# Two mixture-of-experts tile loops: routing tables on partitions, edge scores inside the routing inversion, two shared expert products moved from the head of the second loop to its end

## The reference, cut to what matters

```python
x = x + tanh(g_xattn[0]) * L0_attention(layernorm(x), ctx)          # 1024 rows of 256
x = x + tanh(g_ffn[0])  * L0_moe(layernorm(x))     # 8 experts, inner width 688, top 2 of each row
x = x + tanh(g_xattn[1]) * (0.6*sigmoid(si[:,None] + sj[None,:] + b) + 0.4*layernorm(x))
x = x + tanh(g_ffn[1])  * L1_moe(layernorm(x))     # 15 routed experts, top 2, and one shared expert
# an expert:  silu(x @ w_gate.T) * (x @ w_up.T) @ w_down.T
# shared expert of L1 (inner width 176): applied to every row, added without a routing weight
```

## Time and profile before

| | us |
|---|---|
| median of 3 runs | 369.81 (369.34 to 369.99) |
| the profiled execution, whole | 369.4 |
| its span | 367.4 |
| outside the span (369.4 - 367.4) | 2.0 |
| PE busy in the span | 322.0 (88%) |
| DVE / ACT / POOL busy | 205.4 / 153.1 / 109.4 |
| chain that ended last | PE 76%, DVE 11%, ACT 4%, issue 4%, DMA 2% |

### The profile page before, as it was taken

How to read it: one execution, slowest core, us unless ns; L and a number is a source line. 1 busy time by engine, 2 the same in 40 slices (tenths; PEclk the granted TensorE clock), 3 DMA queues, 4 the chain that set the end, 5 groups by cost and what they waited for, 6 DMA issues and landing times.

```text
span 367.4 us, 6937 instructions
## 1 busy us (share of the span) xinstructions
PE 322.0 (88%) x2144; PEld 185.0 (50%) x2144; DVE 205.4 (56%) x640; ACT 153.1 (42%) x339; POOL 109.4 (30%) x106
## 2 busy tenths in 40 slices
PE   8974599899999999999999999158878999989992
PEld 6643493555555555555555555047334444444440
DVE  1678874655554445555555542495936645455237
ACT  1565402133444343343344444267433545445541
POOL 0021131221333332222212221133234666563310
PEclk9995556999999999999999999655869999999995
DMA  7999919996927372554211112411222222331146
GB/s 236 346 309 319 299 40 287 282 271 199 239 38 245 81 214 41 164 122 133 31 37 14 16 14 29 93 38 59 72 58 55 75 88 87 83 77 58 45 145 228
DMA packets 21146, 48.40 MB, mean 132 GB/s; under 512 B 2600, under 2 KB 11688, under 8 KB 20088
## 3 DMA queue, kind: packets, MB, share of 16 engines
q1 hardware_dynamic: 14680, 35.78, 31.0%
q0 software_dynamic: 6048, 11.28, 14.4%
q10 hardware_dynamic: 384, 0.90, 0.8%
HBM read 37.98 MB, written 9.96 MB: 131 GB/s over the span
## 4 chain that ended last, share of the span: by engine, by line
PE 76%; DVE 11%; ACT 4%; issue 4%; DMA 2%; POOL 1%; ACTq 1%; another core or an unknown queue 1%; DVEq 0%; POOLq 0%
PE bank L1432 27%; PE bank L1406 23%; PE bank L1482 8%; PE bank L1396 6%; PE bank L1245 3%; PE bank L1253 3%; PE bank L1305 2%; DVE st L749 1%; DVE z L939 1%; DMA sums<-y_sb,route_dst 1%; DVE z L827 1%; PE bank L1374 1%; DMA rows<-sums 1%; PE bank L1325 1%; POOL fs L403 1%
## 5 line engine op out<-in xcount | busy, mean ns | idle before, releaser
L1432 PE MATMUL bank<-wgu,xT 128*64 x320 | 99.5, 465 | 1.5 <-issue 0.9
L1432 PE MATMUL bank<-rows,xT 128*64 128x344 f32 x320 | 99.5, 465 | 0.0
L1406 PE MATMUL bank<-wdn,hT 120*64 (+2 forms) x396 | 89.9, 392 | 8.5 <-ACT hT L583 6.8
L1406 PEld LDWEIGHTS bank<-wdn,hT 120*64 120x64 f32 (+1 forms) x396 | 48.9, 140 | 48.4 <-issue 23.0
L1432 PEld LDWEIGHTS bank<-wgu,xT 128*64 128x64 f32 x320 | 43.1, 140 | 47.5 <-issue 8.2
L423 POOL DMA_INDIRECT sums<-y_sb,route_dst x20 | 31.6, 1581 | 115.5 <-ACT y_sb L621 97.5
L415 POOL DMA_INDIRECT x_in<-rows,route_tok x43 | 42.7, 993 | 46.3 <-DVE route_tok L945 17.6
L1019 DVE SCALAR_TENSOR_TENSOR hh<-th,bank 128x344 f32<-128x344 f32 x40 | 20.5, 513 | 58.2 <-ACT th L571 58.2
L1406 PE MATMUL bank<-rows,hT 120*64 120x256 f32 x228 | 52.4, 379 | 0.0
L1432 PEld LDWEIGHTS bank<-rows,xT 128*64 128x64 f32 x320 | 43.1, 140 | 0.0
L571 ACT ACTIVATE th<-bank 128x344 f32<-128x344 f32 x40 | 18.3, 458 | 59.3 <-PE bank L1432 59.3
(11 more groups left out here) (172 smaller groups left out, 451.6 us busy)
## 6 DMA issues: line engine op xcount, KB each, us to landing
wgu<-gu SPq DMA_DIRECT2D x8, 1376.0 KB, 22.4
wdn<-wd SPq DMA_DIRECT2D x8, 720.0 KB, 27.0
wgu<-gu SPq DMA_DIRECT2D x3, 1408.0 KB, 7.1
wdn<-wd SPq DMA_DIRECT2D x5, 576.0 KB, 8.3
rows<-rows SPq DMA_DIRECT2D x8, 256.0 KB, 3.7
wgu<-results SPq DMA_DIRECT2D x4, 512.0 KB, 5.0
wgu<-gu SPq DMA_DIRECT2D x1, 1056.0 KB, 6.8
rows<-xt SPq DMA_DIRECT2D x4, 256.0 KB, 7.4
```

What stands on the lines that cost most here:

```text
L1406: last = mm(psum[7][part, 0:H], hT[0:m.wide, j * P:(j + 1) * P][:, part], wd(j), start=(j == 0), stop=(j == m.chunks - 1))
L1432: last = mm(psum[2 * c + g][part, 0:CH0], xT[:, r, k * P:(k + 1) * P][:, part], w, start=(k == 0), stop=(k == KH - 1))
```

## The change

- `owners` puts the slots' numbers on partitions: one compare of 40x7 (46x14) elements and one sum that writes the integer table; PE, ACT and DVE load an expert's number from the slot's partition.
- Ahead of loop 1, `targets` and `weights` move behind the first staging of weights; the edge scores run between the steps of the inversion in place of the fillers, and `keep_warm(2)` is gone.
- Ahead of loop 2, `owners` comes before the second `hidden_early`; `scale_scores` is split, `shared_terms` stays early and the rest comes later; the second turn of x (`turn_x(1)`) stands ahead of the first slot product; six semaphores for the weights become one.
- `AHEAD = 2`: only row tiles 0 and 1 of the shared expert have their down product at the head. The products of 2 and 3 are kept (`kept_h`) and stand at the end with those of 4 to 7: six downs, in which the turn and copy of the next stand ahead of the down (two banks, two halves `hT1`).
- The results come back by eight DMAs of one row tile each, and `combine` works by row tile, its second instruction waiting for its first.

```diff
@@ owners
-                then(nc.vector.tensor_tensor(
-                    m.scmp[0:1], cf[0:1, C_SLOT:C_SLOT + 2 * m.S].unsqueeze(2).to_broadcast([1, 2 * m.S, E - 1]),
-                    m.incl[0:1, 0:E - 1].unsqueeze(1).to_broadcast([1, 2 * m.S, E - 1]), ALU.is_ge))
-                then(nc.vector.tensor_reduce(out=m.ownf[0:1, :], in_=m.scmp[0:1], axis=X, op=ALU.add))
-                nc.vector.tensor_copy(m.owner[0:1, :], m.ownf[0:1, :]).then_inc(m.experts_ready, 1)
+                halves = 2 * m.S
+                then(nc.vector.tensor_scalar(m.passed[0:halves], m.incl[0:halves, 0:E - 1],
+                                             cf[0:halves, C_ROW:C_ROW + 1], None, ALU.is_le))
+                    nc.vector.tensor_reduce(out=m.owner[0:halves], in_=m.passed[0:halves], axis=X,
+                                            op=ALU.add).then_inc(m.experts_ready, 1)
@@ inverse and what followed it (PE)
-                    if m.n == 0 and i % 2 == 1 and i < 2 * NT - 4:
-                        mm(psum[1][:, 0:D], ones, filler[:, 0:D], start=True, stop=True)
+                    if m.n == 0 and i % 2 == 0:
+                        si = mm(psum[5][:, tile:tile + 1], ctx_all[:, tile * P:(tile + 1) * P], wi, start=True, stop=True)
-            for i in range(NT):
-                last = mm(psum[5][:, i:i + 1], ctx_all[:, i * P:(i + 1) * P], wi, start=True, stop=True)
-            last.then_inc(si_done, 1)
-            keep_warm(2)
@@ head of the second loop (PE)
-            for i in range(2):
-                turn_x(m1, i, i)
-                turn_h(m1, i + 2, i)
-                gate_up_slots(i, i)
-                since(pe, z_copied, i + 2)
-                down_shared(i + 2)
-            turn_x(m1, 2, 2)
+            turn_x(m1, 0, 0)
+            turn_x(m1, 1, 1)
+            gate_up_slots(0, 0)
+            turn_x(m1, 2, 2)
+            gate_up_slots(1, 1)
@@ end of the second loop (PE)
+            def last1(i):
+                if i < NT - 1:
+                    turn_last(i + 1)
+                if NS <= i + 1 < NT - 2:
+                    gate_up_shared((m1.S + i + 1) % 2, xnT[:, i + 3, :])
+                if i == AHEAD:
+                    pe.wait_ge(m1.y_copied, m1.S)
+                pe.wait_ge(z_copied, i)
+                down_shared(m1.S + i)
+            steps(step1, m1.S)
+            for i in range(AHEAD, NT):
+                last1(i)
@@ end (DVE)
+            add_late(AHEAD)
+            hidden(m1, LATE + NS - 2, (LATE + NS) % 2, m1.half)
+            add_late(AHEAD + 1)
+            combine(m1, 0)
+            combine(m1, 1)
+            hidden(m1, LATE + NS - 1, (LATE + NS + 1) % 2, m1.half)
+            for i in range(2, NS):
+                combine(m1, i)
+            add_late(NS)
...
```

More of the change, by code:

```diff
@@ L727, in _ @@
+            def last1(i):
+                if i < NT - 1:
+                    copy_hT(m1, m1.S + i + 1, i % 2)
+                if NS <= i + 1 < NT - 2:
+                    tanh_half(m1, m1.S + i + 3, (m1.S + i + 1) % 2)
+                copy_z(i, m1.S + i)
+            for s in range(m1.S):
+                step1(s, s % RING)
+            for i in range(AHEAD, NT):
+                last1(i)
         @block.vector
@@ L983, in _ @@
             owners(mix[0])
-            targets(mix[0])
-            weights(mix[0])
             def split_shares(m):
@@ L1189, in _ @@
             tokens(m1)
-            scale_scores()
+            owners(m1)
             hidden_early(1)
-            owners(m1)
+            shared_terms()
+            hidden_early(2)
             dve.wait_ge(m1.experts_ready, 1)
-            for n, (_, gu_a, gu_z, dn_a, dn_z) in enumerate(second_weights()):
-                dve.wait_ge(w1_here[n], 16 * (gu_z > gu_a) + 16 * (dn_z > dn_a))
-            hidden_early(2)
+            dve.wait_ge(w1_here, W1_ALL)
             stage_gate_up1(0)
@@ L1522, in down_shared @@
                 down(m1, t, weights, weights)
[L1524 to L1525 removed]
+            for i in range(AHEAD):
+                turn_h(m1, i, i, hh1[:, i, :])
                 since(pe, z_copied, i)
```

225 lines of the change are left out of this document (122 added, 103 removed).

## The result

The changed kernel takes 365.03 us (median of 5 runs, 364.57 to 367.40) where the kernel before takes 369.98 (5 runs, 369.34 to 370.03): a ratio of 0.9875, 95% interval 0.9853 to 0.9896. The ratio makes that 4.6 faster, the two medians lie 4.95 apart; the forecast was 364.4, 5.4 faster. The profiled execution of the changed kernel is the longest of its five (367.4, span 365.3, against a span of 367.4 before). In a second series the same kernel took 364.38 (6 runs) against 368.72 (23 runs), a ratio of 0.9894 (0.9859 to 0.9928), and its profiled execution has a span of 362.5. I call that second trace "the second look" and use both.

What follows compares the result with a forecast made beforehand. PE, 88% busy, was taken to bound the kernel. Terms -1.4 - 5.8 + 0.3 + 1.5 = -5.4 took the profiled 369.4 to 364.0; with the runs' median 0.4 higher, the forecast was 364.4, range 361.8 to 368.2.

Steps and rivals of the forecast that it cites:

- the case I gave most of the chance: Whole kernel: the forecast's own case, a time between 362.8 and 366.0; chance 45%.
- (a): Ahead of loop 1: first product starts earlier without the fillers and the separate edge scores; -1.4, bounds 0.4 to 3.0.
- (b): Ahead of loop 2: quicker `owners`, kept clock and two moved downs bring the third slot product earlier; -5.8, bounds -3.5 to -6.4.
- the 2.3 of clock: Ahead of loop 2: about 2.3 gained if PE's clock stays at 2.4 GHz through the down, slot product and turns.
- hidden of slot tile 0 to 271.85: Head of loop 2: DVE's step for the first slot tile's hidden product, priced to end at 271.85.
- the clock falls anyway: Rival, ahead of loop 2: PE's clock still falls amid short pieces of work; price 2.3, time 366.7; chance 28%.
- The 2.7 of the moved downs: Head of loop 2: two downs and two turns of h only moved to the end; 2.7 of the head's gain.
- Loop 0, last step +0.3: Loop 2: 22 steps of 3.11 unchanged, 0; one more turn ahead of the last step's down, +0.3.
- The slow-loop rival: Rival, loop 2: closer gathers make PE wait for rows, all steps 3.54, 9.5 more, time 373.9; chance 9%.
- (c): Tail: moved downs and unpipelined `combine` lengthen it from 16.7 to 18.2 with DVE as the bound; +1.5.
- The tail blocks itself: Rival, tail: last hidden product behind two `combine` delays PE's last downs if loads come 1.5 later; 366; chance 12%.
- The fillers rival: Rival, head of loop 2: moved downs had filled PE's waits; 367.1, or 369.4 with the clock lost; chance 6%.

Runs made afterwards that it cites:

- seam1: Kernel before, with only the edge scores in place of the inversion's fillers and `targets` and `weights` moved later; 368.53, ratio 0.9993.
- tail2: Changed kernel with `combine` by pairs of tiles and the last hidden product ahead of the first `combine`; 364.13, ratio 0.9870.
- late4: Changed kernel with the fifth and later gathers of loop 2 waiting until the first two slot products are done; 359.41, ratio 0.9844.
- own: Kernel before with only `owners` put on partitions and read from there; 368.46, ratio 0.9987.
- nog: Changed kernel without 16 gathers of loop 2, so later slot tiles use old rows; 360.94, ratio 0.9787.
- gfirst: Changed kernel with POOL issuing the gather for a later tile before the scatter of y in loop 2; 365.21, ratio 0.9885.
- best: Changed kernel with ACT's down-weight staging behind the turned hidden rows' copy, paired `combine`, and last hidden product ahead of the combines; 365.04, ratio 0.9856.
- undo2: Changed kernel with all four shared downs back ahead of loop 2 and both last hidden products ahead of the first `combine`; 368.91, ratio 0.9976.
- undo: Changed kernel with all four shared downs back ahead of loop 2, tail order left as it was; 369.02, ratio 0.9985.

## Why the prediction came out right

The forecast of 364.4 lies 0.6 from the median, and the case I gave most of the chance is the one that happened. Its parts did worse than its sum: the first copy of y in loop 2 starts at 276.84, 5.4 earlier, where 7.2 was forecast.

- **(a) -1.4.** Right in place: the first product came 1.54 earlier (55.02 for a forecast of 55.2). The bounds named a clock that comes back earlier or later; it did neither by rule: "product to y" spreads over 1.5 from one execution to another. Alone, the edit's gain is under what the medians resolve (seam1).
- **(b) -5.8.** Measured -4.1 to -4.2 (19.16 to 15.11 and 14.94). The steps down to the second slot product came as priced: second shared down at 264.92 (266.4 less the 1.4 of (a) is 265.0), taking 1.08 and not 1.97, and slot products of 1.40 and not 2.37, so the 2.3 of clock was won in these two traces. The step that failed is the one behind it, "hidden of slot tile 0 to 271.85", 270.45 with (a): it ends at 272.20, since the first product's signal reached ACT 1.8 late, and everything down to the first copy of y is late with it. Where that signal was late by 0.5 or not at all and the clock stayed, the head takes what was forecast: 13.57 (tail2) and 13.37 (late4), for 19.16 - 5.8 = 13.36. I could have foreseen it, for loop 2 of the kernel before has the same delay. There a product ends at 312.52 by its record, and the tanh behind it starts 1.67 later:

```profile
311.12 1.40 PE L1482 MATMUL bank<-wgu,xT 128*64 x8
...
314.19 0.32 ACT L577 ACTIVATE th<-bank 128x176 f32<-128x176 f32 x1 [1.98 <-remote]
```

  The premise about the clock did not hold either: that the long wait made it fall, and that it stays once the wait is short. In own it falls in a wait of 1.38; in nog, gfirst and best it falls with waits of 0.53 and 0.67, the same as in the changed kernel. The rival "the clock falls anyway", at 28%, is the case in three of eight traces. Its price of 2.3 is right against heads with little or no late signal (13.4 and 13.6 against 15.8 to 16.2), but only 0.7 to 1.3 against the other three (14.9 to 15.1), because no head in which the clock fell ahead of the first product had a late first signal. That the result's own trace kept the full clock is luck. The 2.7 of the moved downs is not measured apart: undo2's head is 2.9 to 3.0 longer, with a fall of the clock in it.
- **Loop 0, last step +0.3.** The second look gives 68.74 for a forecast of 68.7; the first trace has 70.58. Traces of this loop spread by 2.4 under any of the edits, with 5 to 9 long steps. I had read 3.11 as a step's cost; it is 2.93 plus what gathers add (nog). The slow-loop rival, decided from 72 on, did not happen.
- **(c) +1.5.** Measured +1.0 and +1.1 (17.74 and 17.88 for 18.2). DVE's unbroken chain, the single `combine` at 0.92 (0.52 and 0.40) and the last `copy_z` just hidden are as forecast; the first result came some 0.3 sooner behind the last copy of y than priced. "The tail blocks itself" did not happen, with the moved downs there to fill PE's time. Put back at the head, with the tail's order left, it does (undo); with both last hidden products ahead of the first `combine` it does not (undo2).
- **The fillers rival**, that the moved downs cost nothing at the head: refuted by undo and undo2, 3 to 4 by the medians.

An instruction of DVE's tail that waits for the one ahead starts 0.52 behind it (353.37, 353.89), one that doesn't 0.40, both of 0.48, as in the earlier trace rows; paired combines in tail2 take 3.2 for four tiles' worth (351.19 to 354.35) where single ones take 3.7. The prediction weighed a rule of the Trainium skill (VectorE: DVE Perf Modes, "The DRAIN you can't avoid"), by which the next operation waits until the one ahead has drained and a semaphore between two costs nothing extra. The prediction's "never" goes too far: the same section says that an operation that is not held starts earlier, and with that the 0.40 agrees. That a semaphore costs nothing does not agree with the 0.12 between 0.52 and 0.40, and the measurement decides.

Place by place the signs were right. The sum was right partly by luck. In the second look the span is 4.9 shorter for a forecast of 5.4: the 1.6 that (b) fell short is made up by 0.5 in (c), 0.1 in (a) and 0.5 in stretches that no edit touches ("product to y" and what lies between the end of loop 1 and that of the second inversion). The first trace, with its loop of 70.58, is only 2.1 shorter than before.

What gave the gain is shown only in part. Putting the two downs back takes nearly all of it away (undo, undo2), while the owners alone and the first seam alone are not told from no change (own, seam1): at most 1.3 and 1.2 by their intervals.

## What to carry to other kernels

Work that can stand anywhere belongs where the engine that bounds the kernel would otherwise wait: with the two downs at the head the kernel is 3 to 4 us slower, and at the end, where PE has time while DVE combines, they cost nothing that the traces show (tails of 17.74 and 17.88, and 17.75 in undo2). Don't book a fallen clock as the price of one wait: cut several traces of the same program at the same events first, and see how often it falls and what it costs there. And when a consumer starts well behind the recorded end of its producer, look at what else is going on at that moment before looking for a missing dependency.
